# Moving the mixing-matrix steps by one gate part, and weight remainders to GpSimd

## The chip, the cores and the metric

One core of a Trainium2 chip runs the whole kernel. The metric is the time on the device of one execution, in microseconds, as the median of several executions. The profile is of one further execution.

## What is computed

The layer has a recurrent branch and a feed-forward branch over 8 sequences of 512 rows and 512 columns. Cut to what matters here:

```
xn = layernorm(x)                                   # 8 x 512 x 512
x_ssm, z = split(xn @ W_in.T)                       # two times 1024 columns
x_conv = silu(conv4(x_ssm) + conv_b)                # width 4 along the sequence
B, C, dt = split(x_conv @ W_x.T); dt = softplus(dt + mean(dt_bias))
h_t = exp(A*dt_t) * h_{t-1} + dt_t * B_t * x_t      # 16 states for each of 1024 columns
y = (C_t . h_t) + D * x_conv
s = (y * silu(z)) @ out_W.T
out = x + s * silu(feed-forward branch of xn, with an attention that modulates its gate)
```

## The kernel before

The kernel has three stages one after the other: the recurrent branch (the first stage, about the first third of the span), the attention, and the feed-forward part. The change is in the first stage alone. There the loop runs over the 8 sequences, called batches b = 0 to 7.

TensorE multiplies in halves: each float32 operand is split into a high half (rounded to fp32r) and a low half (the operand less its high half), and each product is three matmuls (high by high, high by low, low by high; lines 72 to 74). So each weight is split once: ScalarE copies it into the high tile, and another engine subtracts to get the low tile. The input projection's weights come in four parts c = 0 to 3 of 512 columns (WH and WL; staging W0, which lies in ZS and WS; `split_hi` at L584, `split_lo` at L1018). The out-projection's weights come as two halves (OH and OL; staging OS; `out_hi` at L887, and the subtraction at L1133).

The recurrence isn't run step by step. All of A's rows are equal, so a batch's answer is a product with a 512 by 512 mixing matrix (MH and ML), built from decays and from the B and C rows. For one batch TensorE does, in an order written out by hand in `fast_tensor`:

- the projection of the 8 convolution parts (`project_x`, for batch b+1 while batch b is mixed; for batch 0 ahead of the loop), and after each the two matmuls of `rows` (L659 and L660), which collect B, C and dt in bank PS[5]. They need the low half CL of the part (L993), which VectorE makes after the part's convolution (L985, three instructions);
- the projection of the 8 gate parts (`gate(b, 0)` to `gate(b, 7)`, 12 matmuls each). ScalarE empties each with `gated` into ZS (L860), and a gate part needs the copy of the one two before it, because they take banks 0 and 1 in turn;
- the steps of the mixing matrix, which stand between the gate parts: `rows_turned` (L718), `spread` (L727, which needs RC, written by GpSimd at L1201), `decays` (L736 to L739, which need dt: DTX, LET and DTB of VectorE at L1088 to L1095), `factors_turned` (three groups of four transposes: L747 needs CK of L1118, L752 needs CB2, L756 needs BF1 of L1136), `off_diagonal` (L764 and L769);
- `turned` (L678), then `mix` with the matrix, and `project_out` (L707 to L709).

In batch 0 there is no mixing of an earlier batch to cover the convolutions. Its order is: projection of part 0, part 1, part 2, rows of part 0, part 3, rows of part 1, and so on to part 7, rows of parts 5, 6 and 7, then gate part 0. VectorE goes convolution d+1, low half of part d; ScalarE opens part d+1 (L840), closes part d (Silu at L846, high half CH at L850), with the weight parts 2 and 3 split after the closing of parts 1 and 3.

Each engine runs its own queue in order, and waits are on semaphores that count. `s_wh[c]` and `s_wl[c]` stand for the high and low half of weight part c, `s_oh` and `s_ol` for those of the out-projection. Gate parts 0 and 4 of batch 0 wait for `s_wl[2]` and `s_wl[3]`, and projections 0 and 4 for `s_wl[0]` and `s_wl[1]`. GpSimd does little in this stage: RC once a batch and two small powers.

Of the kernel before, what the change touches and what calls it, by code (L numbers as in the profile page):

```python
# [12 lines left out]
ALU = mybir.AluOpType  # L13
# [19 lines left out]
def build(nc, x, WinT, convw, convb, WxT, Alog, dtb, outWT, Dp, ln1, ln2, WqT, WkT, Wv, Wo, Aw, Bw, WgT, WuT, WdT,  # L33
          ident, umask, arow, maskt, maskT, out):
    ctx = ExitStack()
    with ctx:
# [545 lines left out]
        def split_hi(act, c):  # L582
            act.wait_ge(s_hw[c], 16)
            act.copy(WH[:, :, 512 * c:512 * c + 512], W0[c]).then_inc(s_wh[c], 1)  # L584

        def first_scalar(act):

            act.wait_ge(c_dve, 5)
            split_hi(act, 0)
# [14 lines left out]
        def fast_tensor(pe):  # L604
# [116 lines left out]
            def spread(b):  # L721

                pe.wait_ge(s_r, b + 1)
                if b:
                    pe.wait_ge(s_oc, 4 * (b - 1) + 2)
                for i in range(2):
                    t = pe.matmul(PS[2 + i][:, :], BLK[:, :], RC[:, 512 * i:512 * i + 512], start=True, stop=True,  # L727
                                  skip_group_check=True)
                t.then_inc(s_cb, 1)

            def decays(b):

                p = PS[5]
                pe.wait_ge(s_k, 4)
                pe.wait_ge(s_dt, 7 * b + 6)
                pe.matmul(p[:, 0:64], SBLK[:, :], LET[:, :, :], start=True, stop=True, skip_group_check=True)  # L736
                pe.matmul(p[:, 64:96], UM[:, 1, :], DTX[:, :], start=True, stop=True, skip_group_check=True)
                pe.matmul(p[:, 96:100], STRI[:, :], DTX[:, 28:32], start=True, stop=True, skip_group_check=True)
                pe.matmul(p[:, 100:104], ONE[:, :], DTX[:, 28:32], start=True, stop=True,  # L739
                          skip_group_check=True).then_inc(s_dm, 1)  # L740
# [49 lines left out]
            for b in range(NB):  # L790
                gate(b, 0)
                rows_turned(b)
                gate(b, 1)
                spread(b)
                decays(b)
                gate(b, 2)
                factors_turned(b)
                gate(b, 3)
                off_diagonal(b)
                gate(b, 4)  # L800
                gate(b, 5)
                turned(b, 0)
                gate(b, 6)
                turned(b, 1)
                gate(b, 7)
                if b + 1 < NB:
                    for k in range(4):
                        normed(b + 1, k)
                mix(b, 0)
                for d in range(8):  # L810
                    if d + 2 < 8:
                        turned(b, d + 2)
                    if d + 1 < 8:
                        mix(b, d + 1)
                    if b + 1 < NB:
                        project_x(b + 1, d)
                        if d:
                            rows(b + 1, d - 1)
                    if d:
                        project_out(b, d - 1)  # L820
                    if b == NB - 1:
                        prep_tensor(pe, d)
                project_out(b, 7)
                if b + 1 < NB:
                    rows(b + 1, 7)
# [3 lines left out]
        def fast_scalar(act):  # L829
# [67 lines left out]
            for d in range(8):  # L897
                if d < 7:
                    conv_open(0, d + 1)
                conv_close(0, d)  # L900
                if d in (1, 3):
                    split_hi(act, 2 + d // 2)
            act.wait_ge(s_kv, 4)
            for b in range(NB):
                act.wait_ge(s_ro, 8 * b + 8)
# [2 lines left out]
                if b:  # L908
                    out(b - 1, 0)
                    out(b - 1, 1)  # L910
                if b == 0:
                    out_hi(0)
                gated(b, 0)
                act.wait_ge(s_pn, b + 1)
                act.wait_ge(s_dt, 7 * b)
# [7 lines left out]
                act.activation(ET[:, 3, :], ET[:, 2, :], ACT.Ln).then_inc(s_sa, 1)  # L923
                if b:
                    out(b - 1, 3)
                if b == 0:
                    out_hi(4)
                gated(b, 1)
                act.wait_ge(s_ag, 6 * b + 5)
                act.activation(EX[:, 64:103, :], EX[:, 64:103, :], ACT.Exp).then_inc(s_ex, 1)  # L930
                act.wait_ge(s_ag, 6 * b + 6)
                act.activation(EX[:, 0:64, :], EX[:, 0:64, :], ACT.Exp).then_inc(s_ex, 1)
                gated(b, 2)
                act.wait_ge(s_tr, 3 * b + 2)
                act.wait_ge(s_l2, b)
                act.copy(CBT[:, :], PS[5][0:80, :]).then_inc(s_e2, 1)
                gated(b, 3)
                act.wait_ge(s_l2, b + 1)
                act.wait_ge(s_y, 8 * b)
                act.wait_ge(s_wl[2], 1)  # L940
                for J, (bank, at, n) in enumerate(offd):
                    act.copy(MH[:, J, 128:128 + n], PS[bank][:, at:at + n]).then_inc(s_mh, 1)
                gated(b, 4)
                act.wait_ge(s_g, 7 * b + 7)
                act.copy(MH[:, :, 0:128], PFM[:, :].rearrange("p (c t) -> p c t", c=4)).then_inc(s_mh, 1)
                gated(b, 5)
# [26 lines left out]
        def fast_vector(dve):  # L973
# [38 lines left out]
                dve.wait_ge(s_yh, 8 * b + d + 1)  # L1012
                dve.tensor_tensor(YL[d % 2][:, :], XC[:, d, :], f32(YH[d % 2][:, :]), ALU.subtract).then_inc(s_yl, 1)

            def split_lo(c):
                cols = slice(512 * c, 512 * c + 512)
                dve.wait_ge(s_wh[c], 1)
                dve.tensor_tensor(WL[:, :, cols], W0[c], f32(WH[:, :, cols]), ALU.subtract).then_inc(s_wl[c], 1)  # L1018

            dve.wait_ge(c_ld, 32)  # L1020
            split_lo(0)
            for k in range(4):
                lowered(0, k)
            dve.tensor_reduce(IND[:, :], idn[:, :].rearrange("p (j i) -> p j i", i=16), AX.X, ALU.add).then_inc(s_kc, 1)
# [12 lines left out]
            dve.tensor_scalar(GT[:, :], LEB[:, :], -1.0, 1.0, ALU.mult, ALU.add).then_inc(s_kc, 1)  # L1037
            dve.wait_ge(s_kc, 10)
            dve.tensor_copy(CK[:, 0, :, :], GT[:, 0:7].unsqueeze(2).to_broadcast([128, 7, 16])).then_inc(s_k, 1)
            split_lo(1)  # L1040
            dve.wait_ge(s_kt, 1)
            dve.tensor_copy(STRI[:, :], PS[5][:, 0:128]).then_inc(s_kc, 1)
            dve.tensor_copy(GTM[:, :], PS[5][0:112, 128:256]).then_inc(s_k, 1)
# [14 lines left out]
            for d in range(8):  # L1058
                if d < 7:
                    conv(0, d + 1)  # L1060
                conv_lo(0, d)
                if d == 5:
                    split_lo(2)
            for b in range(NB):
                f, g = 6 * b, 7 * b
                dve.wait_ge(s_pt, b + 1)
# [4 lines left out]
                dve.tensor_reduce(PN[:, :, :], PT, AX.X, ALU.add).then_inc(s_pn, 1)  # L1071

                if b == 0:
                    split_lo(3)
                    fast_deviations(dve, 1, 0)
                    fast_deviations(dve, 1, 1)
                dve.wait_ge(s_sa, 4 * b + 3)
# [50 lines left out]
                if b == 0:  # L1128
                    fast_deviations(dve, 1, 6)
                    fast_deviations(dve, 1, 7)  # L1130
                    for i, k in enumerate((0, 4)):
                        dve.wait_ge(s_oh, i + 1)
                        dve.tensor_tensor(OL[:, k:k + 4, :], OS[:, k:k + 4, :], f32(OH[:, k:k + 4, :]), ALU.subtract).then_inc(s_ol, 1)  # L1133
                dve.wait_ge(s_ex, 2 * b + 2)
                E = EX[:, 0:64, :].rearrange("p (q t) s -> p q t s", q=4)
                dve.tensor_tensor(BF1[:, :, :, :], E[:, :, 15, :].unsqueeze(2).to_broadcast([128, 4, 7, NS]),  # L1136
# [57 lines left out]
            dve.wait_ge(s_yl, 8 * NB)  # L1194

        def fast_pool(pool):
            for b in range(NB):
                pool.wait_ge(s_xo, 3)
                pool.wait_ge(s_pn, b + 1)
                pool.wait_ge(s_l1, b)  # L1200
                pool.tensor_tensor(R4, PN[:, :, 16:32].unsqueeze(2).to_broadcast([128, 4, 16, NS]),  # L1201
                                   PO1[:, :].unsqueeze(1).unsqueeze(3).to_broadcast([128, 4, 16, NS]), ALU.mult).then_inc(s_r, 1)
                if b == 0:
                    fast_powers(pool, 1)
                if b + 2 < NB:
                    fast_powers(pool, b + 2)
            pool.wait_ge(s_pw, 2 * NB)
            pool.wait_ge(s_r, NB)
            prep_pool(pool)
# [1125 lines left out]
```

## Time and profile before

| what | value |
|---|---|
| median of 3 runs | 2586.34 us (2586.32 to 2586.46) |
| profiled execution, its own time | 2587.55 us |
| its span, first to last instruction | 2585.4 us |
| TensorE busy | 2487.2 us (96%) |
| VectorE, ScalarE, GpSimd busy | 1382.6, 1059.4, 439.8 us |
| 0 to 840 us of the span: TensorE, GpSimd busy | 788.95, 35.16 us |

A busy TensorE isn't one at its peak: matmuls overlap, and the time between two starts is what one costs. The idle time ahead of an instruction stands in square brackets in the timelines, with the engine and line that ended it. "issue" is idle time in which the engine waited for nothing that the profile shows.

### The profile page before, as it was taken

Reading aid. Unit: us, or ns where it says so; the run is one execution under the profiler, and the core shown is the slowest. Engines: PE = TensorE matmul, PEld = TensorE weight load, DVE = VectorE, ACT = ScalarE, POOL = GpSimd, SP = SyncE. Lnnn points to the kernel's source line nnn. Section 1 sums busy time; section 2 is a strip of 40 time slices with the busy share of each in tenths; the row PEclk is TensorE's granted clock in tenths of the full one; section 3 lists DMA queues with packets and bytes.
Section 4 is the critical chain, followed back from the end, with each engine's and each line's share of the span. In section 5 each row is a group of like instructions: output and inputs, shape, how many; then the busy total and the mean of one; then the engine's idle time right before and its main releaser. Section 6 shows DMA issues by size and latency. Waiting matters only on the chain.

```text
span 2585.4 us, 38397 instructions
## 1 busy us (share of the span) xinstructions
PE 2487.2 (96%) x14359; PEld 2002.0 (77%) x14359; DVE 1382.6 (53%) x2876; ACT 1059.4 (41%) x1764; POOL 439.8 (17%) x407
## 2 busy tenths in 40 slices
PE   5899999999999899999999899999999999999998
PEld 4678778778788677777777678888888788888887
DVE  6666667567565578888888852212213422222223
ACT  4444444444544367777777641111112211111111
POOL 0000000000000234444443610000000202222222
PEclk8999999999999999999999999999999999999999
DMA  4000000000003577666566411111113312222212
GB/s 140 17 17 17 33 17 17 33 1 33 17 1 103 162 213 207 188 183 185 155 183 184 153 58 49 49 49 49 49 49 110 135 41 97 96 98 95 97 66 82
DMA packets 106972, 228.12 MB, mean 88 GB/s; under 512 B 14976, under 2 KB 15488, under 8 KB 100624
## 3 DMA queue, kind: packets, MB, share of 16 engines
q1 hardware_dynamic: 106528, 225.34, 27.2%
q8 instruction: 120, 1.97, 0.3%
q14 instruction: 68, 0.56, 0.1%
q10 hardware_dynamic: 256, 0.26, 0.0%
HBM read 149.77 MB, written 75.50 MB: 87 GB/s over the span
## 4 chain that ended last, share of the span: by engine, by line
PE 86%; DVE 6%; ACT 3%; issue 3%; DMA 2%; SPq 0%; POOL 0%; DVEq 0%; POOLq 0%; ACTq 0%
PE PS L72 13%; PE PS L74 13%; PE PS L73 13%; PE PS L2122 4%; PE PS L2123 4%; PE PS L2124 4%; PE PS L1622 3%; PE PS L1641 3%; PE PS L1599 2%; PE PS L708 2%; PE PS L707 2%; PE PS L709 2%; PE PS L1601 2%; PE PS L1600 2%; PE PS L693 1%
## 5 line engine op out<-in xcount | busy, mean ns | idle before, releaser
L2191 DVE TENSOR_TENSOR SG<-SG,PS 128x512 f32<-128x512 f32 x124 | 85.2, 687 | 645.4 <-PE PS L74 643.5
L72 PE MATMUL PS<-FH,GU 128*128 128x512 f32 x992 | 387.4, 390 | 1.4 <-DVE DW L2182 1.4
L74 PE MATMUL PS<-FH,GU 128*128 128x512 f32 x992 | 388.3, 391 | 0.0
L73 PE MATMUL PS<-FL,GU 128*128 128x512 f32 x992 | 387.5, 391 | 0.0
L1807 DVE CUSTOM_DVE_ANT_0 PS<-PS,MK 128x512 f32<-128x512 f32 (+3 forms) x512 | 243.8, 504 | 95.2 <-PE PS L1622 94.0
L2161 ACT ACTIVATE SG<-PS 128x512 f32<-128x512 f32 x124 | 74.0, 597 | 467.3 <-PE PS L2098 467.3
L1744 ACT ACTIVATE PF<-PS 128x512 f32<-128x512 f32 (+1 forms) x384 | 199.6, 526 | 84.8 <-PE PS L1643 82.8
L2227 POOL TENSOR_SCALAR XN<-XT,MEAN,RSTD 128x512 f32<-128x512 f32 x32 | 69.5, 2171 | 943.6 <-DMA M<-m_scratch 943.6
L2164 ACT CAST GH<-SG 128x512 fp32r<-128x512 f32 x124 | 76.9, 620 | 351.7 <-DVE SG L2191 351.7
L72 PE MATMUL PS<-XH,WH 128*128 128x512 f32 x512 | 211.1, 412 | 9.9 <-DVE XL L977 9.9
L72 PEld LDWEIGHTS PS<-FH,GU 128*128 128x128 f32 x992 | 186.4, 188 | 42.5 <-issue 1.8
L73 PEld LDWEIGHTS PS<-FL,GU 128*128 128x128 f32 x992 | 186.5, 188 | 41.0
L74 PEld LDWEIGHTS PS<-FH,GU 128*128 128x128 f32 x992 | 186.7, 188 | 39.8
L74 PE MATMUL PS<-XH,WL 128*128 128x512 f32 x512 | 202.3, 395 | 0.0
L73 PE MATMUL PS<-XL,WH 128*128 128x512 f32 x512 | 201.7, 394 | 0.0
L2122 PE MATMUL PS<-DW,GH 128*128 128x512 f32 x500 | 195.8, 392 | 5.6 <-DVE GL L2193 5.6
L2123 PE MATMUL PS<-DW,GH 128*128 128x512 f32 x500 | 195.4, 391 | 0.0
L2124 PE MATMUL PS<-DW,GL 128*128 128x512 f32 x500 | 195.3, 391 | 0.0
L1622 PE MATMUL PS<-KS,QS 96*128 96x512 f32 (+3 forms) x512 | 168.6, 370 | 12.9 <-DVE MX L1807 9.8
L1814 DVE TENSOR_TENSOR PL<-PF,PH 128x1024 f16<-128x1024 f32 (+1 forms) x128 | 177.4, 1386 | 5.7 <-ACT PH L1749 5.7
L1641 PE MATMUL PS<-QS,KS 97*128 97x512 f32 (+3 forms) x512 | 165.1, 353 | 3.5 <-ACT PF L1744 1.9
L1749 ACT CAST PH<-PF 128x1280 f16<-128x1280 f32 x128 | 161.2, 1260 | 4.1
(296 smaller groups left out, 5306.1 us busy)
## 6 DMA issues: line engine op xcount, KB each, us to landing
qk_scratch<-QT SPq DMA_DIRECT2D x128, 256.0 KB, 4.6
QS<-qk_scratch SPq DMA_DIRECT2D x96, 256.0 KB, 4.0
KS<-qk_scratch SPq DMA_DIRECT2D x96, 256.0 KB, 3.9
FH<-rh_scratch SPq DMA_DIRECT2D x16, 1024.0 KB, 5.7
FL<-rl_scratch SPq DMA_DIRECT2D x16, 1024.0 KB, 7.9
XF<-in_x_dram SPq DMA_DIRECT2D x32, 256.0 KB, 3.8
s_scratch<-ZS SPq DMA_DIRECT2D x8, 1024.0 KB, 4.4
rh_scratch<-RH SPq DMA_DIRECT2D x8, 1024.0 KB, 9.6
```

The lines of the kernel that those rows point to most:

```text
L72: pe.matmul(o, lh(k), xh(k), start=open_ and k == 0, stop=False, skip_group_check=True)
L73: pe.matmul(o, lh(k), xl(k), start=False, stop=False, skip_group_check=True)
L74: last = pe.matmul(o, ll(k), xh(k), start=False, stop=close and k == nk - 1, skip_group_check=True)
L1622: t = pe.matmul(p[:, at:at + n], QS[0:96, h, 128 * k:n], KS[0:96, h, 0:n], start=True, stop=True, skip_group_check=True)
L1641: pe.matmul(p[:, at:at + n], KS[0:97, h, 128 * J:128 * J + 128], QS[0:97, h, 128 * J:512], start=True, stop=False, skip_group_check=True)
L1744: act.activation(PE_[u][:, o:o + at], PS[4 + a % 2][:, 0:at], ACT.Exp, scale=SC).then_inc(a_ex, 1)
L1749: act.copy(PH[u][:, :], PE_[u][:, :]).then_inc(a_ph, 1)
L1807: dve.tensor_tensor_reduce(out=p[:, at:at + n], in0=p[:, at:at + n], in1=MK[:, 512 - n:512], scale=1.0, scalar=NEG, op0=ALU.add, op1=ALU.m ...
L1814: dve.tensor_tensor(PL[u][:, 0:n], PE_[u][:, 0:n], PH[u][:, 0:n], ALU.subtract).then_inc(a_rm, 1)
L2122: pe.matmul(PS[4 + k][:, :], GH[g][:, c], DW[:, f, 0, :], start=f == 0, stop=False, skip_group_check=True)
L2123: pe.matmul(PS[4 + k][:, :], GH[g][:, c], DW[:, f, 1, :], start=False, stop=False, skip_group_check=True)
L2124: t = pe.matmul(PS[4 + k][:, :], GL[g][:, c], DW[:, f, 0, :], start=False, stop=f == 7, skip_group_check=True)
```

## The change

1. In `fast_tensor`, for every batch, `decays`, `factors_turned` and `off_diagonal` each come one gate part later. `rows_turned` and `spread` stay. ScalarE's `gated(b, 2)` to `gated(b, 4)` move ahead of the steps that they stood behind.
2. The low halves of weight parts 1 to 3 and both low halves of the out-projection's weights go from VectorE to GpSimd, which does them first of all in its queue, ahead of batch 0's RC. Part 0 stays on VectorE.
3. ScalarE's two `out_hi` go from the head of batch 0 to the convolutions of batch 0, behind the closing of parts 4 and 5.

```diff
+        def split_lo(e, c):
+            cols = slice(512 * c, 512 * c + 512)
+            e.wait_ge(s_wh[c], 1)
+            e.tensor_tensor(WL[:, :, cols], W0[c], f32(WH[:, :, cols]), ALU.subtract).then_inc(s_wl[c], 1)
+
...
                 spread(b)
+                gate(b, 2)
                 decays(b)
-                gate(b, 2)
+                gate(b, 3)
                 factors_turned(b)
-                gate(b, 3)
+                gate(b, 4)
                 off_diagonal(b)
-                gate(b, 4)
                 gate(b, 5)
...
                 if d in (1, 3):
                     split_hi(act, 2 + d // 2)
+                if d in (4, 5):
+                    out_hi(4 * (d - 4))
...
-                if b == 0:
-                    out_hi(0)
                 gated(b, 0)
...
-                if b == 0:
-                    out_hi(4)
                 gated(b, 1)
+                gated(b, 2)
                 act.wait_ge(s_ag, 6 * b + 5)
                 act.activation(EX[:, 64:103, :], EX[:, 64:103, :], ACT.Exp).then_inc(s_ex, 1)
                 act.wait_ge(s_ag, 6 * b + 6)
                 act.activation(EX[:, 0:64, :], EX[:, 0:64, :], ACT.Exp).then_inc(s_ex, 1)
-                gated(b, 2)
+                gated(b, 3)
                 act.wait_ge(s_tr, 3 * b + 2)
                 act.wait_ge(s_l2, b)
                 act.copy(CBT[:, :], PS[5][0:80, :]).then_inc(s_e2, 1)
-                gated(b, 3)
+                gated(b, 4)
...
-                gated(b, 4)
...
-            split_lo(0)
+            split_lo(dve, 0)
...
-            split_lo(1)
...
-                if d == 5:
-                    split_lo(2)
...
-                    split_lo(3)
...
-                    for i, k in enumerate((0, 4)):
-                        dve.wait_ge(s_oh, i + 1)
-                        dve.tensor_tensor(OL[:, k:k + 4, :], OS[:, k:k + 4, :], f32(OH[:, k:k + 4, :]), ALU.subtract).then_inc(s_ol, 1)
...
         def fast_pool(pool):
+            for c in range(1, 4):
+                split_lo(pool, c)
+            for i, k in enumerate((0, 4)):
+                pool.wait_ge(s_oh, i + 1)
+                pool.tensor_tensor(OL[:, k:k + 4, :], OS[:, k:k + 4, :], f32(OH[:, k:k + 4, :]), ALU.subtract).then_inc(s_ol, 1)
```

## Rows read from the trace of the kernel before

**Rows 1.** The page: TensorE and weight loads, and the chain that ended last.

```profile
PE 2487.2 (96%) x14359; PEld 2002.0 (77%) x14359; DVE 1382.6 (53%) x2876; ACT 1059.4 (41%) x1764; POOL 439.8 (17%) x407
...
PE 86%; DVE 6%; ACT 3%; issue 3%; DMA 2%; SPq 0%; POOL 0%; DVEq 0%; POOLq 0%; ACTq 0%
```

**Rows 2.** Busy time by stretch, 100 us in the first stage (one batch).

```profile
200.00:300.00 100.00, 98.60 (x496) 79.92 (x495) 65.48 (x119) 47.86 (x81) 3.98 (x3) 1.00 0.06 22
```

**Rows 3.** Timeline of TensorE, batch 0: start, duration, line, [idle before <- releaser].

```profile
61.58 0.63 PE L659 MATMUL PS<-CH,XP 128*66 128x512 f32 x1 [4.33 <-DVE CL L993]
...
63.93 0.63 PE L72 MATMUL PS<-XH,WH 128*128 128x512 f32 x1
...
67.23 0.41 PE L718 MATMUL PS<-idn,PFM 66*128 66x66 f32 x4
...
72.17 1.98 PE L727 MATMUL PS<-RC,BLK 128*128 128x512 f32 x4 [1.71 <-POOL RC L1201]
...
79.88 0.65 PE L747 MATMUL PS<-idn,CK 128*112 128x128 f32 x4 [2.07 <-DVE CK L1118]
...
87.14 1.10 PE L756 MATMUL PS<-idn,BF 128*112 128x128 f32 x4 [6.17 <-DVE BF L1136]
...
92.82 1.05 PE L764 MATMUL PS<-RC 112*128 112x128 f32 x8
...
100.23 0.60 PE L678 MATMUL PS<-idn,XC 128*128 128x128 f32 x4
```

**Rows 4.** Timeline of TensorE, batch 1.

```profile
183.67 0.41 PE L736 MATMUL PS<-LET,SBLK 128*128 128x64 f32 x2 [0.65 <-DVE DTB L1095]
...
187.91 0.65 PE L747 MATMUL PS<-idn,CK 128*112 128x128 f32 x4 [0.35 <-DVE CK L1118]
...
199.78 0.60 PE L678 MATMUL PS<-idn,XC 128*128 128x128 f32 x4
```

**Rows 5.** Waits of TensorE from 120 to 900 us: total, times, longest.

```profile
PE PS L736 <- DVE DTB L1095: 4.6, 7, 0.7
```

**Rows 6.** Timeline of VectorE, batch 0.

```profile
45.39 0.68 DVE L993 TENSOR_TENSOR CL<-XC,CH 128x512 fp32r<-128x512 f32 x1
46.33 2.31 DVE L985 SCALAR_TENSOR_TENSOR XC<-PS,CW,XC 128x511 f32<-128x511 f32 x3 [0.26 <-ACT XC L840]
...
56.42 2.29 DVE L1018 TENSOR_TENSOR WL<-WS,WH 128x2048 fp32r<-128x2048 f32 x1
...
68.02 2.28 DVE L1018 TENSOR_TENSOR WL<-WS,WH 128x2048 fp32r<-128x2048 f32 x1
...
82.07 4.49 DVE L1133 TENSOR_TENSOR OL<-OS,OH 128x2048 fp32r<-128x2048 f32 x2
```

**Rows 7.** Timeline of ScalarE, batch 0.

```profile
39.79 1.90 ACT L584 CAST WH<-WS 128x2048 fp32r<-128x2048 f32 x1
...
47.37 1.90 ACT L584 CAST WH<-WS 128x2048 fp32r<-128x2048 f32 x1
...
50.91 0.62 ACT L850 CAST CH<-XC 128x512 fp32r<-128x512 f32 x1
```

**Rows 8.** GpSimd's instructions of three lines: duration ns as min/median/max, first and last start.

```profile
L1893 POOL TENSOR_TENSOR GU<-STGC,GU x8: 1261/1278/2422, 1440.1 to 1478.8; 128x512 fp32r<-128x512 f32 x8
...
L1908 POOL TENSOR_TENSOR PL<-PF,PH x112: 667/676/1714, 909.1 to 1433.9; 128x256 f16<-128x256 f32 x112
...
L1201 POOL TENSOR_TENSOR RC<-PN,PO x8: 1961/1966/3866, 68.2 to 776.1; 128x1024 f32<-128x1024 f32 x8
```

**Rows 9.** Timeline of GpSimd in the attention stage.

```profile
1465.59 2.42 POOL L1893 TENSOR_TENSOR GU<-STGC,GU 128x512 fp32r<-128x512 f32 x1
```

**Rows 10.** Timeline of VectorE in the same microseconds.

```profile
1465.10 1.75 DVE L1814 TENSOR_TENSOR PL<-PF,PH 128x1280 f16<-128x1280 f32 x1
1466.78 1.79 DVE L1845 TENSOR_TENSOR GL<-SG,GH 128x512 fp32r<-128x512 f32 x1
```

**Rows 11.** VectorE's subtractions from PSUM in the attention stage: ns, min/median/max.

```profile
L1790 DVE TENSOR_TENSOR QT<-PS,QT x64: 627/679/692, 867.7 to 1425.5; 128x512 fp32r<-128x512 f32 x64
```

More of the change, by code:

```diff
@@ L1013, in mixed_lo @@
                 dve.tensor_tensor(YL[d % 2][:, :], XC[:, d, :], f32(YH[d % 2][:, :]), ALU.subtract).then_inc(s_yl, 1)
[L1015 to L1018, printed above, removed]
             dve.wait_ge(c_ld, 32)
-            split_lo(0)
+            split_lo(dve, 0)
             for k in range(4):
```

## The prediction

> **What bounds the kernel now.** I read the page first: TensorE is busy 96% of the span, and the chain that ended last runs 86% through TensorE [rows 1]. So time is won only where TensorE idles or runs slowly. In the first stage a steady batch is full: 98.60 us of matmuls in 100 [rows 2]. Then I listed what TensorE waits for in the batches after the first. Ahead of the decays it waits 0.7 us for dt, 7 times, 4.6 us in all [rows 5]; ahead of the turned factors it waits 0.35 us in batch 1 [rows 4]. Batch 0 is another matter. From its first gate part at 63.93 to its first turned part at 100.23 pass 36.3 us, in which TensorE waits 1.71, 2.07 and 6.17 us [rows 3]; ahead of it lies a wait of 4.33 us for the low half of a convolved part. I followed each wait to the queue behind it: RC at 72.17 stood behind PN and beside a weight subtraction on VectorE, BF1 at 87.14 behind the two subtractions of the out-projection, 4.49 us [rows 3, 6]. A difference of 0.2% is 5.2 us; that is about what a measurement can tell from no change.
>
> **Steps later, batches 1 to 7.** No instruction is added; the same ones stand one gate part later. The decays move behind gate part 2, about 2.75 us of matmuls, so dt, which was 0.65 us late [rows 4], is there about 2 us early: 0.65 saved. The factors still have one gate part between them and the decays, and what they wait for starts with the decays' result, so their 0.35 us stays. ScalarE now empties gate part 2 before its exponentials; the copy ends near 186.5, and its input EX comes, with the decays 2.1 us later, near 188.3. That is room for the table load of 1.3 us, so nothing is queued up behind it. The off-diagonal part comes 2.1 us later and only one gate part stands behind it; PFM is then whole near 197.6, before the first turned part needs it at 199.78 less 0.65. Sum: 7 times 0.65, 4.6 us [rows 5]. The cover is gate part 5; were it short, turned part 0 would wait.
>
> **Batch 0 from its first gate part on.** Call the start of gate part 0 G (63.93 before). VectorE no longer has the subtraction at 68.02 (2.28 us) and those at 82.07 (4.49 us) [rows 6], ScalarE no longer the two copies of 1.90 us each [rows 7]. Replaying with the durations of before: RC is written in 1.97 us [rows 8] and is ready at G+6.3, where gate part 1 ends; the wait of 1.71 goes. dt is ready near G+8.5 and the decays run at G+11.1, so no wait. VectorE meanwhile does the statistics of batch 1 until G+12.0. CK is ready at G+15.3 and TensorE at G+14.8: a wait of 0.5 for 2.07. BF1 follows after four scalings of rows (1.9 us) at G+18.2, a wait of 1.8 for 6.17. Before, gate part 3 ran slowly behind the long wait, 4.92 us from about 87.9 to 92.82 [rows 3] where about 2.8 is usual; with 1.8 us of idling I take the usual. Sum: 1.7+1.5+4.4+2.1, and 0.3 at the edges: 10.0. Turned part 0 then starts at about G+26.2, where it was G+36.3.
>
> **Where G lands: the five subtractions on GpSimd.** The trace has no GpSimd subtraction of 2048 columns. The nearest are 128x512 into fp32r at 1278 ns and 128x256 at 676 ns [rows 8]: 2.35 ns a column, so 2048 take about 4.9 us. From below, the 1024 columns of RC (operands that repeat) give 1.8 ns a column and 3.9 us; from above, a doubled row (3866 for 1966) gives 9.8 us. I take 4.9, since the first is the same operation on the same types.
>
> Now what they do to VectorE. At 1465.59 GpSimd's subtraction starts while VectorE's of two SBUF operands runs until 1466.85; GpSimd's ends at 1468.01, 2.42 us for 1.28. VectorE's next one, GL, the same form as CL in this stage, starts at 1466.78 and takes 1.79 for 0.69, ending 0.56 after GpSimd's [rows 9, 10]. So who starts first holds the other for the whole instruction. A VectorE subtraction from PSUM isn't held: 64 of them lie between 627 and 692 ns in a stage where GpSimd works [rows 11]; the convolutions L985 read PSUM too, so I leave them unheld.
>
> The Trainium skill says the same in "SBUF — State Buffer", Who interferes with whom: of a VectorE instruction with two SBUF inputs and a GpSimd one that reads SBUF, the second to start blocks fully until the first is done. The trace agrees (1.79 us for 0.69), and by this rule the change pays in the convolutions for what it takes off VectorE.
>
> The replay, with 4.9: weight part 1 lies from 23.8 to 28.7, under TensorE's first projection; no cost. Part 2 starts behind the copy that ends at 41.69 [rows 7], 41.8 to 46.7. It holds CL of part 2, which would start at 45.39 [rows 6], until 46.7, and it ends at 47.2. The convolution at 46.33 starts 0.9 later, so CL of part 3 starts at about 49.46. GpSimd's weight part 3 starts at 49.27+0.08, about 49.35 [rows 7]: a tenth earlier. It holds CL of part 3 until 54.25. TensorE waits 4.2 us for its rows, and convolution 5 starts at 54.8. `out_hi(0)` goes in behind the copy at 50.91, ends near 54.5, and its subtraction on GpSimd runs to 59.6, which holds CL of part 4 until 60.2. Projection 6, slow behind its wait, ends near 59.9; convolution 6 runs to 63.0, CL of part 5 just gets in ahead of the last subtraction (63.7 to 68.6), which then holds CL of part 6 until 69.2. Rows of parts 6 and 7 follow, and G is about 71.0, where it was 63.93: 7.1 lost. The removed subtraction of 2.29 us at 56.42 [rows 6] is already out of this replay. GpSimd is free at 68.6, RC wants it at G+4.3: no cost.
>
> **Sum.** 7.1 lost to G, 10.0 won behind it, 4.6 in the other batches: 7.5 us shorter. The profiled execution took 2587.55 for a span of 2585.4; the span becomes about 2577.9 and that execution 2580.1. The median of the runs, 2586.34, lies 1.2 under it: 2578.8. The attention and the feed-forward part wait for the first stage as a whole, so nothing is given back there.
>
> **The rivals.**
> - CL of part 3 starts first (0.27). My lead is a tenth of a microsecond; a GpSimd subtraction under 4.8 us turns it. Then part 3 on GpSimd runs 50.1 to 54.9 and TensorE's rows of part 3 don't wait; the holds of CL 4, 5 and 6 (1.0, 2.5 and 2.6 us) leave G at about 67.6, 3.7 lost. 3.7-10.0-4.6: 10.9 us shorter, 2575.4. The Trainium skill bears on it: "GPSIMD Engine Reference", Elementwise — side-by-side cycle accounting, has 4497 ns for such an instruction at 2048 columns; by an estimate with that figure it is this branch that comes, and the sum is 10.9. The rows here say 4.9, which is against it.
> - VectorE isn't held in this stage (0.07). Then only the removed 2.29 us counts, less the two copies of 1.90 that delay openings 6 and 7 by about half a microsecond: G is 63.1. 0.85+10.0+4.6: 15.5 us shorter, 2570.9. Against it stand rows 9 and 10.
> - The holds cost more, or the steady batches give less (0.20). If turned part 0 waits where dt did, the 4.6 is gone: 2.9 us shorter. If one more CL is held for a whole subtraction (4.9), 2.6 shorter. If the convolutions are held as well, three holds of 4.9 and one of 3.5 on top of 63.1 give G 81.3: 2.7 us longer. All this lies within 0.2% or near it.
> - Slower (0.04): GpSimd's subtraction takes the doubled price here, 9.8 us. Then VectorE's queue is paced by GpSimd: 41.8 and four times 9.8 is 81.0, and with 4.5 us for the last parts G is 85.5, 21.6 lost: 7.0 us longer, 2593.3. It decides from 8.1 us an instruction on. Against it: the long rows of GpSimd end a fixed time after VectorE's, which is waiting and not a slower rate.
> - The forecast itself: 0.42.
>
> **How the numbers follow.** The predicted time is 2578.8. The range reaches from short of the unheld case to the case in which the steady gain is lost: 2572.5 to 2584.0; outside lie the unheld case and most of the heavier holds, about 2 in 10. The likeliest case with its own uncertainties (2 us for each hold) goes from 2576.5 to 2581.5. Faster by over 0.2% (below 2581.2): 0.38 of the forecast's 0.42, all of the next two (0.34), 0.03 of the fourth: 0.75. Slower 0.04; within 0.2% 0.21.
>
> **What would show it.** In the changed profile: GpSimd's five subtractions near 4.9 us each, the first starting near 23.8. CL (L993's successor) of parts 2, 3, 4 and 6 at 1.9 to 5.4 us instead of 0.68, each ending 0.56 behind a GpSimd subtraction; which of CL 3 and weight part 3 starts first tells the first two cases apart. G at 71.0, turned part 0 at 97.3 where it was 100.23. No wait at the decays in batches 1 to 7, and the 0.35 at the factors still there, a batch 0.65 shorter. The prediction is wrong if GpSimd's subtractions cost other than 3.9 to 6, if instruction fetches in the first 30 us (VectorE and ScalarE stand still there, and the code is laid out anew) move the start by microseconds, or if turned part 0 meets PFM late.

## The result, and the profile after

The changed kernel takes 2572.84 us (median of 5 runs) where the one before takes 2586.46 in the same rounds; the ratio is 0.9943, with a 95% interval from 0.9929 to 0.9957. One of the five executions, 3453.74 us at a granted clock of 0.653, is left out of the ratio; the median of the other four is 2571.61. So the change is worth 14.85 us by these four, and between 11 and 18 by the interval, where 7.5 was forecast, and 2571.61 lies below the stated range, which began at 2572.5. The sign was right, the size was not, and it was the second case, not the first, that came. The profiled execution took 2574.06 us for a span of 2571.9, 13.5 less than before.

The page after, TensorE's row and the shares of the chain, which answer to [rows 1]:

```profile
PE 2484.1 (97%) x14359; PEld 2001.8 (78%) x14359; DVE 1376.2 (54%) x2871; ACT 1060.4 (41%) x1764; POOL 458.8 (18%) x412
...
PE 88%; DVE 6%; issue 3%; ACT 2%; DMA 1%; SPq 0%; POOL 0%; DVEq 0%; POOLq 0%; ACTq 0%
```

TensorE's work is the same (x14359); its share rises because the span is shorter. A steady batch by stretch, beside [rows 2], is fuller: 99.25 us in 100 for 98.60.

```profile
200.00:300.00 100.00, 99.25 (x501) 80.85 (x499) 66.71 (x122) 48.82 (x83) 3.98 (x3) 1.00 0.08 27
```

The timeline of TensorE in batch 0, the places of [rows 3] (lines moved by five or so: L664 are the rows, L723 the turned rows, L732 the spread, L752 and L761 two of the turned factors, L683 turned part 0; an x1 or x3 where an x4 stood before means that the view ended there):

```profile
64.58 0.69 PE L664 MATMUL PS<-CH,XP 128*66 128x512 f32 x1 [4.25 <-DVE CL L996]
...
66.35 0.63 PE L72 MATMUL PS<-XH,WH 128*128 128x512 f32 x1
...
70.13 0.41 PE L723 MATMUL PS<-idn,PFM 66*128 66x66 f32 x4
...
73.18 1.98 PE L732 MATMUL PS<-RC,BLK 128*128 128x512 f32 x4
...
81.97 0.65 PE L752 MATMUL PS<-idn,CK 128*112 128x128 f32 x4 [0.42 <-DVE CK L1112]
...
84.82 0.65 PE L761 MATMUL PS<-idn,BF 128*112 128x128 f32 x4 [1.77 <-DVE BF L1127]
...
92.75 0.49 PE L683 MATMUL PS<-idn,XC 128*128 128x128 f32 x3
```

Gate part 0 starts at 66.35, 2.4 later than before. From there to turned part 0 pass 26.4 us where 36.3 passed [rows 3]; the waits of 1.71, 2.07 and 6.17 are 0, 0.42 and 1.77. Turned part 0 is 7.5 earlier. In batch 1 (beside [rows 4]) the wait ahead of the decays is gone and the one for CK stayed. The spread of batch 1 before, then batch 1 after:

```profile
181.05 1.97 PE L727 MATMUL PS<-RC,BLK 128*128 128x512 f32 x4
```

```profile
173.56 1.97 PE L732 MATMUL PS<-RC,BLK 128*128 128x512 f32 x4
174.97 0.80 PE L72 MATMUL PS<-XH,WH 128*128 128x512 f32 x1
...
178.12 0.33 PE L741 MATMUL PS<-LET,SBLK 128*128 128x64 f32 x2
...
182.28 0.32 PE L752 MATMUL PS<-idn,CK 128*112 128x128 f32 x1 [0.38 <-DVE CK L1112]
```

The turned rows of batches 1 to 7 start at 178.00, 277.56 and so on to 775.13 before, and at 170.51, 269.18 to 762.48 after: a batch is 99.52 before and 98.66 after, 0.86 shorter. The 13.5 us are these two: 7.5 in batch 0 and 6.0 in the seven others. From the last turned part to the end pass 1746.9 us in both.

What the change costs shows where GpSimd and VectorE meet. Timeline of GpSimd, then of VectorE (L996 makes CL, the first row here that of part 2), beside [rows 6]:

```profile
41.56 4.61 POOL L589 TENSOR_TENSOR WL<-WS,WH 128x2048 fp32r<-128x2048 f32 x1 [15.40 <-ACT WH L584]
49.12 4.92 POOL L589 TENSOR_TENSOR WL<-WS,WH 128x2048 fp32r<-128x2048 f32 x1 [2.95 <-ACT WH L584]
54.06 9.92 POOL L1192 TENSOR_TENSOR OL<-OS,OH 128x2048 fp32r<-128x2048 f32 x2
```

```profile
45.16 1.56 DVE L996 TENSOR_TENSOR CL<-XC,CH 128x512 fp32r<-128x512 f32 x1
46.65 2.30 DVE L988 SCALAR_TENSOR_TENSOR XC<-PS,CW,XC 128x511 f32<-128x511 f32 x3
48.87 0.68 DVE L996 TENSOR_TENSOR CL<-XC,CH 128x512 fp32r<-128x512 f32 x1
51.04 2.31 DVE L988 SCALAR_TENSOR_TENSOR XC<-PS,CW,XC 128x511 f32<-128x511 f32 x3 [1.49 <-ACT XC L845]
53.27 1.31 DVE L996 TENSOR_TENSOR CL<-XC,CH 128x512 fp32r<-128x512 f32 x1
54.69 2.32 DVE L988 SCALAR_TENSOR_TENSOR XC<-PS,CW,XC 128x511 f32<-128x511 f32 x3
56.92 2.67 DVE L996 TENSOR_TENSOR CL<-XC,CH 128x512 fp32r<-128x512 f32 x1
...
61.74 3.39 DVE L996 TENSOR_TENSOR CL<-XC,CH 128x512 fp32r<-128x512 f32 x2
```

CL of part 2 starts at 45.16, while GpSimd's second subtraction runs until 46.17, and ends at 46.72, 0.55 behind it. The convolutions at 51.04 and at 54.69 (three instructions each) take 2.31 and 2.32 while GpSimd works; the one at 46.65, which falls between two subtractions, takes 2.30. They are not held. CL of part 3 starts at 48.87, 0.25 us ahead of GpSimd's third subtraction at 49.12, takes its 0.68, and it is GpSimd that is held (4.92 for 4.6). That order is what the forecast had the other way round.

### The profile page after: what moved, and what is told of

The parts are those of the page before. It is cut to its first block, busy times and chain, and to the rows that moved or that the text cites. A ratio compares the mean times of both kernels' runs of the same rounds, so it can differ in the third digit from the quotient of the medians.

```text
span 2571.9 us, 38397 instructions
## 1 busy us (share of the span) xinstructions
PE 2484.1 (97%) x14359; PEld 2001.8 (78%) x14359; DVE 1376.2 (54%) x2871; ACT 1060.4 (41%) x1764; POOL 458.8 (18%) x412
## 3 DMA queue, kind: packets, MB, share of 16 engines
q8 instruction: 120, 1.97, 0.3%
## 4 chain that ended last, share of the span: by engine, by line
PE 88%; DVE 6%; issue 3%; ACT 2%; DMA 1%; SPq 0%; POOL 0%; DVEq 0%; POOLq 0%; ACTq 0%
PE PS L72 14%; PE PS L74 13%; PE PS L73 13%; PE PS L2118 4%; PE PS L2120 4%; PE PS L2119 4%; PE PS L1618 3%; PE PS L1637 3%; PE PS L1595 3%; PE PS L713 2%; PE PS L712 2%; PE PS L714 2%; PE PS L1597 2%; PE PS L1596 2%; PE PS L698 1%
```

## The experiments

For each kernel the profile gives where the first stage stands, and the rounds give the time. Ahead of the first convolution nothing is changed, yet the first rows of part 0 start between 37.83 and 39.36 from one execution to the next (38.90 before, 38.69 in the changed kernel). So the marks of batch 0 are counted from there: "gate" is the time from the first rows to gate part 0, "turned" that to turned part 0, and "part 0" is how long gate part 0 itself took, from its start to the turned rows of batch 0. "CL" are the durations for parts 2 to 6 (a pair where the profile merges parts 6 and 7), "batch" is the time between the turned rows of batches 1 and 2. All in us. Each ratio is to the kernel before in the same rounds, whose medians lie between 2584.57 and 2586.46.

| kernel | CL of parts 2, 3, 4, 5, 6 | gate | part 0 | turned | batch | median | ratio to before |
|---|---|---|---|---|---|---|---|
| before | 0.68 each | 25.03 | 3.30 | 61.33 | 99.56 | 2586.46 | 1 |
| changed | 1.56, 0.68, 1.31, 2.67, pair 3.39 | 27.66 | 3.78 | 54.06 | 98.67 | 2571.61 (of four) | 0.9943 (0.9929 to 0.9957) |
| steps alone | 0.68 each | 25.03 | 4.55 | 61.06 | 98.66 | 2576.47 | 0.9964 (0.9950 to 0.9978) |
| subtractions alone | 1.55, 0.68, 1.31, 2.68, pair 3.39 | 27.64 | 3.81 | 58.77 | 99.57 | 2581.60 | 0.9987 (0.9978 to 0.9996) |
| high halves alone | 0.68 each | 25.47 | 4.28 | 61.70 | 99.53 | 2586.49 | 0.9999 (0.9990 to 1.0008) |
| out-projection's on VectorE | 1.53, 0.68, 1.30, 0.68, 0.68 | 25.52 | 4.61 | 52.77 | 98.67 | 2571.85 | 0.9947 (0.9933 to 0.9960) |
| memset, hidden | 1.57, 0.68, 1.31, 2.68, pair 3.38 | 27.66 | 3.35 | 55.24 | 98.67 | 2572.16 | 0.9949 (0.9936 to 0.9963) |
| memset, in the way | 1.96, 4.96, 4.78, 4.97, 0.68 | 34.82 | 3.61 | 61.07 | 98.67 | 2579.40 | 0.9976 (0.9967 to 0.9985) |
| zeros | 0.68 each | 24.08 | 5.12 | 51.86 | 98.66 | 2568.83 | 0.9933 (0.9919 to 0.9947) |
| in four pieces | 0.77, 0.68, 0.99, 1.55, pair 3.46 | 25.77 | 4.37 | 52.75 | 98.68 | 2570.48 | 0.9941 (0.9927 to 0.9954) |
| both remedies | 0.76, 0.68, 1.02, 0.68, 0.68 | 24.44 | 4.75 | 51.82 | 98.66 | 2570.11 | 0.9941 (0.9927 to 0.9954) |
| changed, once more | 1.56, 0.68, 1.30, 2.67, pair 3.39 | 27.67 | 3.94 | 54.25 | 98.68 | 2572.96 | 0.9957 (0.9943 to 0.9970) |

A single time tells less: where only five runs stand in a ratio its interval is 3.6 us to either side, and from the last turned part to the end, in a part of the program that is the same in all, pass between 1744.1 us (high halves alone) and 1748.2 (out-projection's on VectorE). So the marks carry the comparisons, and the times are asked only whether they agree.

The column "part 0" matters for reading "turned". The twelve matmuls of gate part 0 are the same in every kernel and stand ahead of all moved steps, but they come behind TensorE's wait for the last low halves, in which the granted clock falls to its lower level, 1.2 GHz (0.50 from 62 to 64 us in the changed kernel, 1.00 from 58 to 60). In the kernel with zeros all twelve run at that level, 0.43 from start to start:

```profile
62.17 0.63 PE L72 MATMUL PS<-XH,WH 128*128 128x512 f32 x1
62.60 0.63 PE L73 MATMUL PS<-XL,WH 128*128 128x512 f32 x1
...
67.29 0.43 PE L723 MATMUL PS<-idn,PFM 66*128 66x66 f32 x4
```

In the changed kernel five of them do and the others follow at 0.23. From the end of gate part 0 to turned part 0 pass 22.6 us in the changed kernel and in every kernel that keeps both edits, but for the hidden memset (24.2). So in these kernels turned part 0 gains less than gate part 0 does, and the difference lies in gate part 0: the four with fewer holds start it earlier (24.08 to 25.77), and 8 to 12 of the twelve run at the low level. Some of it is scatter as well: executions in which TensorE had nearly the same waits up to there took 3.78, 3.94 and 3.35 (changed, once more, hidden memset), and 3.30 and 4.55 (before, steps alone). What makes the clock rise when it does is left open.

**Steps alone.** The kernel before with the reordered gate parts and nothing else:

```diff
                 spread(b)
+                gate(b, 2)
                 decays(b)
-                gate(b, 2)
+                gate(b, 3)
                 factors_turned(b)
...
```

> The mixing-matrix steps one gate part later, nothing else. Theory (the steps' gain is a wait of 0.65 us a batch plus the drain and refill around it, 0.86 us in the changed profile): batches 1 to 7 give 6.0 us; in batch 0 the subtractions on VectorE still set BF1, so turned part 0 comes only about 1 us earlier than 100.23: 7 us shorter in all. Rival (only the wait of 0.65 goes, the rest of the 0.86 comes from the moved subtractions): 4.6 us in batches 1 to 7, 5.6 in all.

A batch takes 98.66, as in the changed kernel: all of the 0.86 comes from the order, and the rival with 0.65 falls. Batch 0 gives next to nothing, 0.3 (61.06 for 61.33; the 98.97 in the profile for 100.23 is mostly an earlier start). But 1.25 was lost in gate part 0 (4.55 for 3.30), ahead of anything that was moved; from its end on turned part 0 comes 1.5 sooner (31.48 for 33.00), near the 1 that was expected. The wait for CK falls from 2.07 to 0.38, but BF1 still stands behind the out-projection's subtractions, the wait for it is 6.18, and the slow clock behind it lasts longer (5.86 us from L756 to the off-diagonal part for 5.68). The ratio 0.9964 is 9.3 us, between 5.7 and 12.9, and holds the 7 that was expected.

**Subtractions alone.** The changed kernel with the steps put back:

```diff
                 spread(b)
-                gate(b, 2)
                 decays(b)
-                gate(b, 3)
+                gate(b, 2)
                 factors_turned(b)
...
```

> The low halves on GpSimd and the high halves of the out-projection among the convolutions, the steps where they were. Theory: gate part 0 starts near 66.4 as in the changed kernel, turned part 0 near 95.7 (4.5 us earlier than 100.23; the wait for CK grows to about 2.9, that for BF1 is 1.8), nothing in the other batches: 4.5 to 5 us shorter. Rival (the two edits simply add up): 13.6 less what the steps alone give, 6.5 us or more.

Turned part 0 comes 2.6 earlier than before and not 4.5; a batch takes 99.57, unchanged. The ratio says 3.4 us (1.0 to 5.7). The two edits don't add up: in batch 0 they give 0.3 and 2.6 alone and 7.3 together (1.5, 5.7 and 10.4 from the end of gate part 0 on). Alone, each leaves TensorE a long wait behind which the clock is low: 6.18 for BF1 with the steps alone, 2.75 for CK here. The changed kernel is 4.7 ahead of this one, with the same 27.6 to gate part 0. Where that is shows in the waits of TensorE from 60 to 101 us and in the stretches of 81 to 91:

```profile
PE PS L752 <- DVE CK L1112: 2.7, 1, 2.7
PE PS L761 <- DVE BF L1127: 1.1, 1, 1.1
```

```profile
81.00:86.00 5.00, 2.82 (x13) 2.32 (x14) 4.97 (x13) 2.21 (x4) 0.00 (x0) 0.63 0.00 0
86.00:91.00 5.00, 5.00 (x21) 4.10 (x19) 4.51 (x8) 0.59 (x1) 0.00 (x0) 0.69 0.00 0
```

The same two stretches of the changed kernel, with waits of 0.42 and 1.77:

```profile
81.00:86.00 5.00, 2.81 (x19) 1.99 (x18) 4.97 (x14) 2.12 (x4) 0.00 (x0) 1.00 0.00 0
86.00:91.00 5.00, 5.00 (x29) 3.79 (x28) 4.90 (x9) 1.51 (x4) 0.00 (x0) 1.00 0.01 2
```

The third figure from the end is the granted clock: 0.63 and 0.69 with the steps in their old place, 1.00 with the new. From L761 to the off-diagonal part, with one gate part between them in both, pass 5.21 us (84.93 to 90.14) for 3.24 (84.82 to 88.06). So 2.0 of the 4.7 is the clock behind L761. The other 2.7 is one gate part. L761 starts at the same time in both, 46.15 and 46.13 after the first rows, because VectorE writes BF1 at the same time in both (45.47). With the steps in their old place three gate parts are still to come behind it, with the new place two: from the off-diagonal part to turned part 0 pass 7.41 and 4.69 us. The shorter waits (2.75, 1.11 and 0.16 at the decays, for 0.42 and 1.77) are the same gate part seen from TensorE, and nothing to be added. That is what moving the steps does in batch 0: it puts a gate part in front of a result that comes from VectorE when it comes.

**High halves alone.** The kernel before, with `out_hi` behind the closing of parts 4 and 5:

```diff
                 if d in (1, 3):
                     split_hi(act, 2 + d // 2)
+                if d in (4, 5):
+                    out_hi(4 * (d - 4))
...
```

> Only ScalarE's two copies of the out-projection's weights among the convolutions; all else as before. Theory: they delay openings 6 and 7 by up to half a microsecond each and free nothing that TensorE waits for: turned part 0 within 0.7 us of 100.23, the same time as before within 1 us. Rival: their old place was on the path to dt, 2 us or more shorter.

Nothing, or 0.4 lost: 61.70 for 61.33, ratio 0.9999. Gate part 0 starts 0.44 later, as the delayed openings had it; it takes 1.0 longer (4.28 for 3.30), and the slow stretch behind BF1 is 1.1 shorter (4.62 for 5.68), both by the clock. From PN to the last of dt (DTB) pass 5.33 us on VectorE where 5.34 passed, so the old place of the copies was not on the path to dt. This part of the change only makes the high halves ready for GpSimd.

**Out-projection's on VectorE.** The changed kernel, with the two subtractions of OL taken from GpSimd:

```diff
             for d in range(8):
                 if d < 7:
                     conv(0, d + 1)
                 conv_lo(0, d)
+            for i, k in enumerate((0, 4)):
+                dve.wait_ge(s_oh, i + 1)
+                dve.tensor_tensor(OL[:, k:k + 4, :], OS[:, k:k + 4, :], f32(OH[:, k:k + 4, :]), ALU.subtract).then_inc(s_ol, 1)
...
                 split_lo(pool, c)
-            for i, k in enumerate((0, 4)):
...
```

> The changed kernel with the out-projection's two subtractions back on VectorE, behind the convolutions, where it stands idle for 5.4 us. Theory (GpSimd's subtractions hold VectorE's CL of parts 5 and 6): CL of parts 5 and 6 at 0.68 us, gate part 0 near 64.0 in place of 66.35, turned part 0 near 90.5 in place of 92.75: 2.3 us shorter than the changed kernel, about 15.9 shorter than before. Rival (the holds are covered, ScalarE's copies set the end of the convolutions): gate part 0 where it was, and 4.5 us on VectorE may delay PN: same as the changed kernel or slower.

CL of parts 5 and 6 is back at 0.68 and gate part 0 comes 2.1 earlier than in the changed kernel, as the theory had it. The 4.49 us on VectorE lie in its idle time: PN waits 1.62 for TensorE all the same. Turned part 0 gains 1.3 on the changed kernel, less than the 2.3, since gate part 0 took 0.8 longer (4.61 for 3.78). The time, 2571.85, doesn't tell the two apart.

**The order of two starts.** GpSimd fills a tile of 128x448 that nothing reads at that time, between its first and second subtraction. In the first try it waits for nothing:

```diff
             for c in range(1, 4):
+                if c == 2:
+                    pool.memset(BF1[:, :, :, :], 0.0)
                 split_lo(pool, c)
```

> The changed kernel with one GpSimd memset of 128x448 (about 0.46 us) between its first and second subtraction, if it doesn't fit into the idle time there (it waits for nothing, so it may run early; then nothing changes). Theory (who starts first holds the other; the lead of CL of part 3 is 0.25 us): if the second subtraction comes 0.4 us later, the third starts ahead of CL of part 3, CL takes about 5 us, gate part 0 lies near 70 and the kernel is 3.4 us longer than the changed one. Rival: the order doesn't matter, at most 0.5 us longer. If the memset is hidden, the run tells only how much the changed kernel scatters.

It ran at 25.96, in idle time, and told nothing of the order. It told something else: with the same waits as the changed kernel (0.43 and 1.77) the clock fell here, 0.78 in the stretch of 81 to 86 us, and the gate part behind took 4.85 us from 83.53 (with the transposes) where the changed kernel takes 3.24 from 84.82. That is 1.6 us of scatter between two runs of the same work on TensorE. At turned part 0 1.2 of it is left (55.24 for 54.06), because gate part 0 happened to take 0.4 less. In the second try the memset waits for the second high half:

```diff
             for c in range(1, 4):
+                if c == 2:
+                    pool.wait_ge(s_wh[2], 1)
+                    pool.memset(BF1[:, :, :, :], 0.0)
                 split_lo(pool, c)
```

> As the run before with the memset of 128x448, now behind the wait for the second high half, so that it can't run early: GpSimd's second subtraction comes 0.49 us later. Theory (who starts first holds the other): it ends near 46.7 in place of 46.2, CL of part 2 near 47.3, and GpSimd's third subtraction (49.1) now starts ahead of CL of part 3 (49.4), which is held to about 54.3; gate part 0 near 69.5 in place of 66.35, about 3 us longer than the changed kernel in the first stage. Rival (order doesn't matter, each waits its share): gate part 0 at most 0.5 later.

Its timelines of GpSimd and of VectorE:

```profile
41.74 0.47 POOL L1191 MEMSET BF<- 128x448 f32 x1 [14.47 <-ACT WH L584]
42.17 4.61 POOL L589 TENSOR_TENSOR WL<-WS,WH 128x2048 fp32r<-128x2048 f32 x1
49.33 4.55 POOL L589 TENSOR_TENSOR WL<-WS,WH 128x2048 fp32r<-128x2048 f32 x1 [2.55 <-ACT WH L584]
56.26 4.55 POOL L1195 TENSOR_TENSOR OL<-OS,OH 128x2048 fp32r<-128x2048 f32 x1 [2.38 <-ACT OH L892]
63.36 4.55 POOL L1195 TENSOR_TENSOR OL<-OS,OH 128x2048 fp32r<-128x2048 f32 x1 [2.56 <-ACT OH L892]
```

```profile
45.37 1.96 DVE L996 TENSOR_TENSOR CL<-XC,CH 128x512 fp32r<-128x512 f32 x1
...
49.48 4.96 DVE L996 TENSOR_TENSOR CL<-XC,CH 128x512 fp32r<-128x512 f32 x1
...
56.58 4.78 DVE L996 TENSOR_TENSOR CL<-XC,CH 128x512 fp32r<-128x512 f32 x1
...
63.50 4.97 DVE L996 TENSOR_TENSOR CL<-XC,CH 128x512 fp32r<-128x512 f32 x1
```

GpSimd's third subtraction now starts 0.15 ahead of CL of part 3, at 49.33 against 49.48, and CL is held for all of it. A memset of 0.47 us makes gate part 0 7.2 later (34.82 for 27.66), not 3, and the kernel 7.8 us slower (2579.40 for 2571.61; the four runs of the changed one lie at 2569.53 to 2574.06, these eleven at 2578.01 to 2582.95). ScalarE's timeline shows why (L845 opens part 5, L892 makes the first high half of the out-projection):

```profile
52.43 0.78 ACT L845 ACTIVATE XC<-PS,CB,CW 128x512 f32<-128x512 f32 x1 [3.18 <-PE PS L74]
...
54.29 1.90 ACT L892 CAST OH<-OS 128x2048 fp32r<-128x2048 f32 x1
```

The reason for the 7.2, as these timelines read, is that the order keeps itself: a held CL delays TensorE's rows and the next projection, ScalarE waits for that projection before it opens the part, and so before it makes the next high half; GpSimd's next subtraction then starts 0.32 ahead of the next CL (56.26 against 56.58), and the one after 0.14 ahead (63.36 against 63.50). GpSimd's subtractions aren't slowed here: 4.55 each.

**Zeros in place of the subtractions.** GpSimd writes zeros in place of the low halves of its five subtractions, so that these are left out of the result:

```diff
             for c in range(1, 4):
-                split_lo(pool, c)
+                pool.wait_ge(s_wh[c], 1)
+                pool.memset(f32(WL[:, :, 512 * c:512 * c + 512]), 0.0).then_inc(s_wl[c], 1)
...
```

> The changed kernel, but GpSimd writes zeros to the four low halves (weight parts 1 to 3 and the out-projection's) instead of reading and subtracting, so those low halves are left out of the result. Theory (the holds of CL cost what batch 0 doesn't gain ahead of gate part 0): every CL at 0.68, gate part 0 near 62.7 in place of 66.35, turned part 0 near 89.1, 3.6 us shorter than the changed kernel in the first stage; the price of all holds. Rival (the convolutions' own beat sets it): gate part 0 within 1 us of 66.35.

Every CL takes 0.68, and from the first rows to gate part 0 pass 24.08 us for 27.66. So the holds of the changed kernel cost 3.6 us at gate part 0, as expected, and 2.2 at turned part 0; the other 1.4 is gate part 0 at the low clock (5.12 for 3.78). Whether GpSimd would hold VectorE by writing alone is not shown: none of these memsets (1.8 us each) ran beside a CL.

**In four pieces.** Each subtraction on GpSimd as four of 512 columns:

```diff
-                split_lo(pool, c)
+                pool.wait_ge(s_wh[c], 1)
+                for k in range(4):
+                    cols = slice(512 * c, 512 * c + 512)
+                    t = pool.tensor_tensor(WL[:, k, cols], W0[c][:, k, :], f32(WH[:, k, cols]), ALU.subtract)
+                t.then_inc(s_wl[c], 1)
...
```

> The changed kernel with each of GpSimd's five subtractions cut into four of 128x512 (about 1.28 us each, 5.1 for 4.6). Theory (a hold lasts to the end of one GpSimd instruction): no CL over 0.68+1.3; CL of part 5 at 2.67 and the pair of parts 6 and 7 at 3.39 shrink by 1 us and more, gate part 0 near 64.5, about 1.5 us shorter than the changed kernel in the first stage. Rival (VectorE gets in only when GpSimd's queue is empty): the holds stay or grow, gate part 0 later than 66.35.

The holds shrink (0.77 for 1.56, 0.99 for 1.31, 1.55 for 2.67) and gate part 0 comes 1.9 earlier, though four pieces take 5.0 us where one takes 4.6. The pair of parts 6 and 7, 3.46, did not shrink: each of the two is now held once (1.77 and 1.76). A hold lasts to the end of one instruction, not of the queue; the rival falls.

**Both remedies**, and the changed kernel beside it in the same rounds. The edit is the last one for the weights' three subtractions, and for the out-projection's two that of the kernel with them on VectorE:

```diff
             for c in range(1, 4):
-                split_lo(pool, c)
+                pool.wait_ge(s_wh[c], 1)
+                for k in range(4):
...
                 conv_lo(0, d)
+            for i, k in enumerate((0, 4)):
+                dve.wait_ge(s_oh, i + 1)
...
```

> A version drawn from the runs before: GpSimd's three weight subtractions in four pieces each, and the out-projection's two on VectorE behind the convolutions. Theory: CL of part 2 near 0.8 and of part 4 near 1.0 us, those of parts 5 to 7 at 0.68, gate part 0 near 63.0 (62.2 with no hold at all, 64.0 and 64.2 with one of the two remedies), turned part 0 near 90.4: about 2 us shorter than the changed kernel in the first stage. Rival (each remedy had already taken the whole of the gain): gate part 0 at 64, no better than either.

> The changed kernel once more, on the chip and in the rounds of the version above. Theory: the order of the starts (CL of part 3 0.25 us ahead of GpSimd's third subtraction) holds in each run, so the time is 2570 to 2574 again. Rival (the order flips from run to run and makes the scatter): some runs near 2579, as with the delayed subtraction.

VectorE's timeline in the version with both:

```profile
44.37 0.76 DVE L996 TENSOR_TENSOR CL<-XC,CH 128x512 fp32r<-128x512 f32 x1
...
51.67 1.02 DVE L996 TENSOR_TENSOR CL<-XC,CH 128x512 fp32r<-128x512 f32 x1
...
61.29 4.49 DVE L1061 TENSOR_TENSOR OL<-OS,OH 128x2048 fp32r<-128x2048 f32 x2
67.54 0.43 DVE L1069 TENSOR_REDUCE PN<-PS 128x132 f32<-128x264 f32 x1 [1.77 <-PE PS L723]
```

Gate part 0 comes 3.2 earlier than in the changed kernel and turned part 0 2.2 earlier, as early as with no hold at all. Its five runs lie at 2568.97 to 2571.50, those of the changed kernel at 2572.01 to 2575.53: 2.9 us between the medians, and the two sets don't overlap. By its marks it is the fastest kernel here that computes everything. The highest of the changed kernel's nine runs, these five and the four above, is 2575.53, well short of 2579, and its CL of part 3 leads again by 0.25 (49.53 against 49.78): its scatter isn't the order flipping.

## Why the prediction was wrong

**The price of GpSimd's subtraction was the step that failed.** The prediction took 2.35 ns a column from the difference of two rows, 1278 ns at 512 columns and 676 at 256 [rows 8], and got 4.9 us for 2048. It took 4.54 to 4.61. The two rows differ in more than their length: one writes fp32r, the other f16, and from one operation alone, a piece of 512 (5.0 for four) and the whole of 2048 (4.55), it is 2.15 ns a column and not 2.35. A line through two different instructions was good to 7%, and the case hung on 2%: the lead was put at a tenth of a microsecond, the wrong way round. With 4.61 the second subtraction ends early enough for CL of part 3 to start 0.25 ahead. The memset bears this out: with it the second subtraction ended at 46.78, where the replay had 46.7, and GpSimd then led by 0.15, as the replay had it.

The Trainium skill had the better number: "GPSIMD Engine Reference", Elementwise — side-by-side cycle accounting, gives 4497 ns for a tensor_tensor of 2048 float32 columns. The trace agrees within 2.5% (4.54 to 4.61), and so does the branch that the prediction tied to that figure.

**So the second case came, with 0.27 and not with 0.42.** Its own sum was 10.9, and 13.5 was measured in the profile: 1.3 less was lost ahead of gate part 0, and 1.4 more was won in the other batches. The terms:

| term | second case | measured |
|---|---|---|
| gate part 0 | 3.7 later | 2.4 later (2.6 from the first rows) |
| from there to turned part 0 | 10.0 shorter | 9.9 shorter |
| batches 1 to 7 | 4.6 shorter | 6.0 shorter |

The holds of CL of parts 4, 5 and 6 were put at 1.0, 2.5 and 2.6 and were 0.6, 2.0 and 2.0 (1.31, 2.67 and 3.39 for two, less 0.68 each).

**Steps later, batches 1 to 7: right in kind, short in size.** The wait at the decays went and the one at CK stayed (0.38), both as said. But 0.65 a batch was only what the profile calls idle. The spread's four matmuls took 2.62 us to the start of the decays before, 1.97 of them busy and 0.65 idle [rows 4]; with a gate part behind them the next matmul starts 1.41 us after the spread does (173.56 to 174.97). A matmul's end in the trace is modelled, and when the next one is ready the two overlap. Some of that comes back in the first matmul of the gate part, 0.63 to the next start; 0.21 a batch stays. The steps alone show the same 98.66.

**Batch 0 behind gate part 0: right.** RC without a wait, CK 0.42 (0.5 said), BF1 1.77 (1.8 said), the gate part behind at full clock; 26.4 for 26.2. That full clock was taken and not argued. It held in the changed kernel and in six of the seven other kernels that keep both edits, and fell in one, where the gate part took 1.6 longer. How near 26.4 came is in part luck: gate part 0, which the forecast left as it was, took from 3.35 to 5.12 in these kernels by the clock, and where the rest took the same 22.6 the sum lay between 26.3 and 27.8.

**That who starts first holds the other: right.** CL is held to 0.55 behind GpSimd's end each time, convolutions never. The rival that VectorE isn't held had gate part 0 0.85 earlier than before; with the zeros and no hold it is 0.95 earlier (24.08 for 25.03). Turned part 0 is there 9.5 earlier, with the 6.0 of the other batches 15.5, which is what the rival said; the ratio says 17.3 (13.7 to 20.9). So the rival had its own sum right and only its condition wrong. The Trainium skill's rule ("SBUF — State Buffer", Who interferes with whom) of full blocking by the first to start agrees with 4.96 us for 0.68.

**Had the first case come, its parts would have been off too.** Forced by the memset, gate part 0 lay at 73.70 where the prediction said 71.0: it let CL of part 5 in ahead of the last subtraction, and in the run GpSimd led each time. With 6.0 for the other batches in place of 4.6 the time would still have been close, 2579.4 for 2578.8; two misses that nearly cancel.

What stays open is the scatter between the runs of one kernel, from 2.5 us (five runs with both remedies) to 8.8 (21 runs of the kernel before, 2582.98 to 2591.78). Part of it is the clock in batch 0 (up to 1.2 in gate part 0 and 1.6 behind BF1 between executions with the same waits), part lies in the attention and the feed-forward part (1744.1 to 1748.2); what moves those wasn't looked for.

## What to carry to other kernels

When work goes to GpSimd beside a busy VectorE, list the VectorE instructions with two SBUF inputs in that stretch and who starts first at each: a lead of 0.25 us was worth 7 us here. Keep GpSimd's instructions short or put them where VectorE works from PSUM, and look for idle time on VectorE itself first; 4.5 us of subtractions cost nothing in a gap of 5.4. If a forecast hangs on which of two instructions starts first by a tenth of a microsecond, say that there are two outcomes, and price the operation from the same operation or not at all.

## What the runs showed of the hardware that was not expected

- Such a meeting took two courses, each of them again and again (2569.5 to 2575.6 us in nine executions, 2578.0 to 2583.0 in eleven). A delay of 0.47 us on GpSimd grew to 7.2 us at gate part 0, because each hold set up the next.
- A TensorE stall of the same length, 1.77 us, behind one of 0.42 or 0.43, left the clock at 1.00 in the changed kernel and brought it to 0.78 in the stretch of 81 to 86 us in another with the same work, which made the next gate part 1.6 us longer.
- Gate part 0, behind TensorE's wait for the last low halves, takes 3.30 to 5.12 us for the same twelve matmuls, as three to twelve of them run at the clock's lower level. Of the 3.6 us that the holds cost at its start, 1.4 did not reach turned part 0 for this reason.
- Removing a wait of 0.65 us on TensorE gave 0.86: the idle time in the trace starts at a modelled end.
